# Second cross attention: score products first, three pieces, and the values of a step in one product

## The chip, the core and the metric

The kernel runs on one core of a Trainium2 chip. The metric is the time of one execution on the device, in microseconds; lower is better. The core has a matrix engine (TensorE, PE in the profile; its weight loads are listed apart as PEld), VectorE (DVE), ScalarE (ACT), GpSimd (POOL) and SyncE (SP, which issues transfers). Each runs its own instructions in order and waits for the others through semaphores. TensorE writes its results into PSUM, eight banks of 512 float32 columns on 128 partitions.

## What is computed

The reference is a decoder of two layers on 2048 rows of 256 numbers, with a context of 1601 rows of 192. Each layer has self attention, cross attention to the context and a feed-forward part, each followed by a layer norm of the sum. The change concerns the cross attention of the second layer:

```python
q = x @ w_q + b_q
k = context @ w_k + b_k
v = context @ w_v + b_v
q = q.reshape(B, Lq, N_HEADS, HEAD)   # 16 heads of 16
...
scores = jnp.einsum('bqhd,bkhd->bhqk', q, k) * scale
weights = jax.nn.softmax(scores, axis=-1)
out = jnp.einsum('bhqk,bkhd->bqhd', weights, v).reshape(B, Lq, D)
return out @ w_o + b_o
```

## The kernel before

The stages run one after the other; the second cross attention is `l1_cross_heads` (line 1105). It treats the 16 heads as 8 pairs and the 2048 queries as two halves, which makes 16 "halves" `u`, each for two heads and 1024 queries. A half runs through 13 steps `kt`, one for each block of up to 128 context rows. The two heads of a pair lie in partitions 0 to 63 and 64 to 127 of the stacked queries and keys `sq` and `sk`, so products of the two heads use different halves of TensorE's rows.

A softmax needs the maximum of each row of scores first. The kernel computes the scores twice: once with queries on the partitions, in pieces of 400 or 402 columns that VectorE reduces to a negative maximum, and once transposed, with the context on the partitions and the negative maximum as one more row of the stacked queries, so that ScalarE can take the exponential directly. The pieces of a half are computed during the half before it. A step of the loop thus has this work:

- two score products (`scores`, line 1371), one for each group of 512 queries, each of two matmuls (one per head), into two buffers `pST` of two banks each;
- two exponentials by ScalarE (line 1552) from `pST` into `pr`, which has three buffers;
- the value product of the step before (`values`, line 1386): four matmuls of 32 columns of weights, which stand side by side in the array and add into one bank `pO`;
- four or five score pieces (`maximum`, line 1319), each into one of the three banks `pM`, each reduced by VectorE (line 1433). 64 pieces belong to a half; the first step of a half has four, the others five. They run ahead by 64 + 12 pieces, so the last half and the end of the one before have none left;
- now and then a full-array unit, which uses all rows and columns and also takes a bank `pM`: the projections of the second half of the queries and keys (line 1296, in halves 4 and 5; ScalarE copies them at line 1534 and VectorE subtracts at line 1424), one normalisation per half (transposes at line 1331, in the step `kt` = 3), transposes and products of the output projection (lines 1341 and 1350), and a transposition of the maxima (`shift`, line 1325), which stands among the pieces and after which SyncE moves the row into the stacked queries.

Nothing is scheduled at run time. `units_in` (line 1123) gives the units of a step and their order, and TensorE, VectorE and ScalarE all go through the same lists. Every unit has a number in this order, its bank is the number modulo 3, and TensorE waits, before it writes a bank, until the unit three numbers before has been read out:

```python
def unit(name):
    if number[name] >= 3:
        pe_.wait_ge(s_free[number[name] % 3], number[name] // 3)
```

Because engines run in order, whatever stands behind such a wait in TensorE's program waits as well. The order of a step on TensorE is written out at the end of the tensor block: the first score product, two pieces, the second score product, the first 256 columns of the values, two pieces, the other 256 columns, the full-array units, the remaining pieces.

The first cross attention (`l0_cross_heads`) has the same plan with 8 pairs of heads of 64; its value product (line 930) has 512 columns and two column tiles of 64.

Of the kernel before, what the change touches and what calls it, by code (L numbers as in the profile page):

```python
# [1104 lines left out]
def l1_cross_heads(nc, A, G, sems):  # L1105

    H, HD, W = 16, 16, 32
    KV = CTX + 1
    ROWS = 64
    STEPS = NC_  # L1110
    HALVES = H
# [10 lines left out]
    def maxima_in(u, kt):  # L1122

        before = done(u, kt - 1) if kt else done(u - 1, STEPS - 1)
        return range(before, done(u, kt))

    def units_in(u, kt):

        whole = []
        if u == 4 and kt >= 6 and kt % 2 == 0:  # L1130
            whole.append(("q", 1, kt // 2 - 3))
        if u == 5 and kt < 8 and kt % 2 == 0:
            whole.append(("k", 1, kt // 2))
        if u >= 1 and kt == 3:
            whole.append(("norm", u - 1))
        if 9 <= u < 13 and kt in (5, 7, 9):
            whole.append(("turn", 0, u - 9) if kt == 5 else ("out", 0, u - 9, (kt - 7) // 2))
        if u == HALVES - 1 and kt >= 5 and kt < 11:
            whole.append(("turn", 1, kt // 8) if kt in (5, 8) else ("out", 1, kt // 8, (kt - 6) % 3))
        parts = []  # L1140
        for i in maxima_in(u, kt):
            parts.append(("max", i))
            if i % MX == 5 and i > MX:
                parts.append(("shift", i // MX - 1))
        if u == HALVES - 2 and kt == STEPS - 1:
            parts.append(("shift", HALVES - 1))
        return parts[:2], parts[2:4], whole, parts[4:]

    def units_of(u, kt):

        return [name for names in units_in(u, kt) for name in names]
# [14 lines left out]
    with ExitStack() as ctx:  # L1166
# [6 lines left out]
        v1 = m.sb("x1v", [P, NC_, H, W])  # L1173
# [5 lines left out]
        pr = [m.sb(f"x1pr{i}", [P, 4, QG]) for i in range(3)]  # L1179
# [11 lines left out]
        pO = m.ps("x1pO", [P, QG])  # L1191
        s_in, s_wq, s_bias, s_wv, s_one, s_vset = m.sem("x1_in"), m.sem("x1_wq"), m.sem("x1_bias"), m.sem("x1_wv"), m.sem("x1_onesrow"), m.sem("x1_vset")
        s_full, s_free = [m.sem(f"x1_slotfull{i}") for i in "012"], [m.sem(f"x1_slotfree{i}") for i in "012"]
        s_st, s_ex, s_pv, s_oc = m.sem("x1_scores"), m.sem("x1_exp"), m.sem("x1_values"), m.sem("x1_outcopied")
# [20 lines left out]
        def rows(kt):  # L1215
            return min(P, CTX - kt * P)
# [7 lines left out]
        with nc.Block() as block:  # L1224
# [64 lines left out]
            def _(pe_):  # L1289
# [65 lines left out]
# [3 lines that stand above are left out]
                    {"q": project, "k": project, "v": project_v, "max": maximum, "shift": shift, "norm": norm,  # L1358
                     "turn": turn, "out": out}[name[0]](name)

                def scores(u, kt, g):
                    if kt == 0 and g == 0:
                        pe_.wait_ge(s_sh, 32 * (u + 1))
                    q, k = sq[u // 2 % 2], sk[u // 2 % 2]
                    c = (u % 2) * 1024 + g * QG
                    n = 2 * (u * STEPS + kt) + g
                    if n >= 2:
                        pe_.wait_ge(s_ex, n - 1)
                    for a in range(2):
                        part = slice(64 * a, 64 * a + ROWS)  # L1370
                        mm = nc.tensor.matmul(pST[n % 2][0:rows(kt), a, :], k[part, kt * P:kt * P + rows(kt)],  # L1371
                                              q[part, c:c + QG], start=True, stop=True)
                    mm.then_inc(s_st, 1)

                def values(n, part):
                    u, kt = n // STEPS, n % STEPS
                    c = slice(256 * part, 256 * part + 256)
                    pe_.wait_ge(s_ex, 2 * n + 2)
                    if kt == 0:
                        if u == 0:  # L1380
                            pe_.wait_ge(s_vset, 2 + NC_)
                        else:
                            pe_.wait_ge(s_oc, u)
                    r = rows(kt)
                    for q4 in range(4):
                        mm = nc.tensor.matmul(pO[W * q4:W * q4 + W, c], v1[0:r, kt, u // 2 * 2 + q4 // 2, :],  # L1386
                                              pr[n % 3][0:r, q4, c], start=(kt == 0 and part == 0),
                                              stop=(kt == STEPS - 1 and part == 1))
                    if part == 1:
                        mm.then_inc(s_pv, 1)  # L1390

                for name in first + first_maxima:
                    unit(name)
                for u in range(HALVES):
                    for kt in range(STEPS):
                        front, middle, whole, rest = units_in(u, kt)
                        scores(u, kt, 0)
                        for name in front:
                            unit(name)
                        scores(u, kt, 1)  # L1400
                        if u or kt:
                            values(u * STEPS + kt - 1, 0)
                        for name in middle:
                            unit(name)
                        if u or kt:
                            values(u * STEPS + kt - 1, 1)
                        for name in whole + rest:
                            unit(name)
                values(HALVES * STEPS - 1, 0)
                values(HALVES * STEPS - 1, 1)  # L1410
                for name in last:
                    unit(name)

# [1 line left out]
            def _(dve):  # L1415
# [61 lines left out]
                def added(name):  # L1477
                    _, half, c, b = name
                    t = 4 * c + 2 * b
                    wait_filled(dve, name)  # L1480
                    if half == 0:
                        dve.wait_ge(s_res, t + 2)
                    else:
                        wait_emptied(dve, ("out", 0, c, b))
                    both = G.xN[:, t:t + 2, :].rearrange("p t d -> p (t d)")
                    emptied(nc.vector.tensor_tensor(both, bank(name)[:, :], both, ALU.add), name)
# [38 lines left out]
            def _(act):  # L1525
# [35 lines left out]
                def turned_rows(name):  # L1561
                    _, half, c = name
                    wait_filled(act, name)
                    if half or c >= 2:
                        wait_filled(act, ("out", half, c - 2, 1) if c >= 2 else ("out", 0, c + 2, 1))
                    emptied(nc.scalar.activation(turned[c % 2][:, :], bank(name)[:, :], ACT.Copy), name)
# [1424 lines left out]
```

## Time and profile before

| | us |
|---|---|
| median of 3 runs | 3449.01 |
| lowest and highest run | 3447.76, 3451.31 |
| the profiled execution, first to last instruction | 3459.0 |
| TensorE busy (share of the span) | 3138.3 (91%) |
| VectorE busy | 2354.6 (68%) |
| ScalarE busy | 1708.5 (49%) |
| GpSimd busy | 1731.8 (50%) |

The profile is of one execution on the chip. Its page gives busy times and the costliest groups of instructions; the trace behind it can be asked for the timeline of a stretch, the waits (who waited for whom) and the busy times of each engine in a stretch. L1319 is line 1319 of the kernel. A row of the timeline merges neighbouring instructions of the same kind: "2.50 DVE ... x5" are five instructions that took 2.50 us from the start of the first to the end of the last. In brackets stands how long the engine was idle before, and what it waited for; "issue" is time in which it waited for nothing that the profile shows. A matmul in float32 is recorded as two. The ends of matmuls are modelled, so starts are the safer marks.

### The profile page before, as it was taken

Reading aid. Unit: us, or ns where it says so; the run is one execution under the profiler, and the core shown is the slowest. Engines: PE = TensorE matmul, PEld = TensorE weight load, DVE = VectorE, ACT = ScalarE, POOL = GpSimd, SP = SyncE. Lnnn points to the kernel's source line nnn. Section 1 sums busy time; section 2 is a strip of 40 time slices with the busy share of each in tenths; the row PEclk is TensorE's granted clock in tenths of the full one; section 3 lists DMA queues with packets and bytes.
Section 4 is the critical chain, followed back from the end, with each engine's and each line's share of the span. In section 5 each row is a group of like instructions: output and inputs, shape, how many; then the busy total and the mean of one; then the engine's idle time right before and its main releaser. Section 6 shows DMA issues by size and latency. Waiting matters only on the chain. (4 is left out here: it accounts for less than half of the span.)

```text
span 3459.0 us, 62575 instructions
## 1 busy us (share of the span) xinstructions
PE 3138.3 (91%) x24201; PEld 1810.0 (52%) x24201; DVE 2354.6 (68%) x4987; ACT 1708.5 (49%) x2102; POOL 1731.8 (50%) x1163
## 2 busy tenths in 40 slices
PE   7999999989999999999999953958989999999797
PEld 3666666644555555555555523846654434444346
DVE  5999999945655665566656556156429978888518
ACT  3888888823434444444444441222234656666641
POOL 5999999814777777777777831322460000000012
PEclk9999999989999999999999976988997999999898
DMA  2000000020000000000000054730021111120101
GB/s 70 6 2 2 2 2 2 26 55 1 4 1 4 1 4 4 1 4 1 4 1 1 1 160 136 239 86 1 1 43 18 18 18 18 18 26 10 33 1 37
DMA packets 65530, 91.51 MB, mean 26 GB/s; under 512 B 9586, under 2 KB 55539, under 8 KB 64371
## 3 DMA queue, kind: packets, MB, share of 16 engines
q1 hardware_dynamic: 61682, 83.17, 9.5%
q0 software_dynamic: 3072, 4.34, 0.7%
q8 instruction: 194, 3.18, 0.4%
q14 instruction: 70, 0.57, 0.1%
q10 hardware_dynamic: 512, 0.26, 0.0%
HBM read 62.34 MB, written 10.65 MB: 21 GB/s over the span
## 5 line engine op out<-in xcount | busy, mean ns | idle before, releaser
L969 DVE TENSOR_REDUCE x0hm<-x0pM 128x1 f32<-128x400 f32 (+1 forms) x1024 | 520.8, 563 | 378.3 <-PE x0pM L871 378.2
L434 POOL TENSOR_SCALAR rows<-rows,mb 128x1024 bf16<-128x1024 bf16 x512 | 567.5, 1119 | 98.1 <-DVE mb L382 98.1
L376 DVE TENSOR_SCALAR_CACHE_REDUCE rows<-pS 128x1024 bf16<-128x1024 f32 x512 | 605.8, 1209 | 2.0 <-PE pS L312 1.5
L445 ACT ACTIVATE prT<-pP 128x1024 bf16<-128x1024 bf16 x512 | 521.9, 1024 | 110.1 <-PE pP L323 92.6
L1433 DVE TENSOR_REDUCE x1hm<-x1pM 128x1 f32<-128x400 f32 (+1 forms) x1024 | 519.1, 567 | 67.4 <-PE x1pM L1319 64.2
L1552 ACT ACTIVATE x1pr<-x1pST 128x1024 f32<-128x1024 f32 (+1 forms) x416 | 403.8, 1022 | 216.1 <-PE x1pST L1371 216.0
L831 POOL TENSOR_TENSOR x0acc<-x0acc,x0pr 128x1024 f32<-128x1024 f32 (+1 forms) x176 | 422.1, 2398 | 110.2 <-ACT x0pr L1080 95.0
L831 POOL TENSOR_TENSOR x0acc<-x0acc,o_nat 128x1024 f32<-128x1024 f32 (+1 forms) x176 | 419.1, 2381 | 72.3 <-ACT o_nat L1080 53.5
L1080 ACT ACTIVATE x0pr<-x0pST 128x1024 f32<-128x1024 f32 (+1 forms) x208 | 212.9, 1024 | 279.6 <-PE x0pST L915 279.6
L1080 ACT ACTIVATE o_nat<-x0pST 128x1024 f32<-128x1024 f32 (+1 forms) x208 | 213.0, 1024 | 278.4 <-PE x0pST L915 278.0
L2666 POOL MEMSET f_tri<- 128x128 f32 x1 | 0.2, 209 | 675.7 <-POOLq L1224 675.7
L1319 PE MATMUL x1pM<-x1sk,x1sq 64*128 64x400 f32 (+1 forms) x1024 | 322.1, 443 | 15.0 <-DVE x1ql L1424 4.1
L323 PE MATMUL pP<-ident_b,rows 128*128 128x128 bf16 x4096 | 318.8, 221 | 0.9 <-ACT prT L445 0.5
L323 PEld LDWEIGHTS pP<-ident_b,rows 128*128 128x128 bf16 x4096 | 231.1, 98 | 116.5 <-POOL rows L434 86.0
L871 PE MATMUL x0pM<-x0kh,x0qh 64*128 64x400 f32 (+1 forms) x1024 | 279.7, 368 | 11.5 <-ACT x0v L1090 4.0
L1319 PEld LDWEIGHTS x1pM<-x1sk,x1sq 64*128 64x128 f32 x1024 | 153.6, 191 | 228.1 <-issue 143.7
L1386 PE MATMUL x1pO<-x1pr,x1v 128*32 128x256 f32 (+1 forms) x3328 | 264.2, 393 | 0.4 <-ACT x1pr L1552 0.4
L1371 PE MATMUL x1pST<-x1sq,x1sk 64*128 64x512 f32 (+1 forms) x832 | 258.2, 447 | 3.1 <-ACT x1pr L1552 1.6
L312 PE MATMUL pS<-kT,qT 64*128 64x512 bf16 x1024 | 200.5, 389 | 45.2 <-DVE rows L376 30.0
L915 PE MATMUL x0pST<-x0qh,x0kh 64*128 64x512 f32 (+1 forms) x832 | 222.6, 448 | 0.0
L930 PE MATMUL x0pO<-x0pr,x0v 128*64 128x512 f32 (+1 forms) x832 | 210.8, 604 | 0.1
L930 PE MATMUL x0pO<-o_nat,x0v 128*64 128x512 f32 (+1 forms) x832 | 210.6, 604 | 0.0
(367 smaller groups left out, 5125.2 us busy)
## 6 DMA issues: line engine op xcount, KB each, us to landing
m_w<-in_moe_w1T SPq DMA_DIRECT2D x16, 1024.0 KB
m_w<-in_moe_w2T SPq DMA_DIRECT2D x16, 1024.0 KB, 9.1
acc_d<-m_zero SPq DMA_DIRECT2D x8, 514.0 KB, 9.5
m_acc<-acc_d SPq DMA_DIRECT2D x8, 514.0 KB, 5.6
x1sq<-x1qh SPq DMA_DIRECT2D x32, 128.0 KB, 4.0
x1sk<-x1kh SPq DMA_DIRECT2D x32, 100.1 KB, 3.6
rows_d<-m_xr SPq DMA_DIRECT2D x1, 2176.0 KB, 9.0
g_xN<-in_x SPq DMA_DIRECT2D x1, 2048.0 KB
```

Source lines behind the costliest of these rows:

```text
L323: mm = nc.tensor.transpose(pP[half][:, k, :], rows[u][:, kt * P:(kt + 1) * P], G.ident_b[:, :])
L376: nc.vector.tensor_scalar(rows[u][:, half * 1024:(half + 1) * 1024], pS[half][:, :], 1.0, None, ALU.mult, ALU.max, accum_out=mx[u][:, half ...
L434: nc.gpsimd.tensor_scalar(r, r, -1.0, mb[u][:, 0:1], ALU.mult, ALU.add).then_inc(s_df, 1)
L445: nc.scalar.activation(prT[u][:, half * 8:(half + 1) * 8, :], pP[half][:, :, :], ACT.Exp, scale=-1.0 / HD ** 0.5).then_inc(s_ex, 1)
L831: nc.gpsimd.tensor_tensor(total[0:r, :, :], total[0:r, :, :], pr[n % NP][0:r, :, :], ALU.add)\
L871: filled(nc.tensor.matmul(bank(name)[:, 0:w], qh[g % 3][half, t * P:(t + 1) * P], kh[g // 4 % 2][half, c0:c0 + w], start=True, stop=True), ...
L930: mm = nc.tensor.matmul(pO[64 * a:64 * a + 64, :], v_all[0:r, kt, c:c + HD], pr[n % NP][0:r, a, :], start=(kt == 0), stop=(kt == NK - 1))
L969: emptied(nc.vector.tensor_reduce(hm[g % 2][:, a, t, i % 8 // 2:i % 8 // 2 + 1], bank(name)[:, 0:w], AX.X, ALU.max, negate=True), name)
L1080: nc.scalar.activation(pr[n % NP][0:r, :, :], pST[n % 2][0:r, :, :], ACT.Exp, scale=HD ** -0.5)\
L1319: filled(nc.tensor.matmul(bank(name)[:, 0:w], q[part, c:c + P], k[part, c0:c0 + w], start=True, stop=True), name)
L1433: emptied(nc.vector.tensor_reduce(hm[u % 2][:, a, t, i % 8 // 2:i % 8 // 2 + 1], bank(name)[:, 0:w], AX.X, ALU.max, negate=True), name)
L1552: nc.scalar.activation(pr[step % 3][0:r, g::2, :], pST[n % 2][0:r, :, :], ACT.Exp, scale=HD ** -0.5).then_inc(s_ex, 1)
```

## The change

On TensorE a step becomes: both score products, three pieces, the full-array units, the values of the step before in one product of 512 columns, the remaining pieces. The order of the units in a step, and with it the banks and the order on VectorE and ScalarE, changes accordingly: a full-array unit now comes after the third piece of its step and not after the fourth.

```diff
@@ units_in
-        return parts[:2], parts[2:4], whole, parts[4:]
+        return parts[:3], whole, parts[3:]
@@ tensor block
-                def values(n, part):
+                def values(n):
                     u, kt = n // STEPS, n % STEPS
-                    c = slice(256 * part, 256 * part + 256)
                     pe_.wait_ge(s_ex, 2 * n + 2)
...
                     for q4 in range(4):
-                        mm = nc.tensor.matmul(pO[W * q4:W * q4 + W, c], v1[0:r, kt, u // 2 * 2 + q4 // 2, :],
-                                              pr[n % 3][0:r, q4, c], start=(kt == 0 and part == 0),
-                                              stop=(kt == STEPS - 1 and part == 1))
-                    if part == 1:
-                        mm.then_inc(s_pv, 1)
+                        mm = nc.tensor.matmul(pO[W * q4:W * q4 + W, :], v1[0:r, kt, u // 2 * 2 + q4 // 2, :],
+                                              pr[n % 3][0:r, q4, :], start=(kt == 0), stop=(kt == STEPS - 1))
+                    mm.then_inc(s_pv, 1)
...
-                        front, middle, whole, rest = units_in(u, kt)
+                        front, whole, back = units_in(u, kt)
                         scores(u, kt, 0)
-                        for name in front:
-                            unit(name)
                         scores(u, kt, 1)
-                        if u or kt:
-                            values(u * STEPS + kt - 1, 0)
-                        for name in middle:
+                        for name in front + whole:
                             unit(name)
                         if u or kt:
-                            values(u * STEPS + kt - 1, 1)
-                        for name in whole + rest:
+                            values(u * STEPS + kt - 1)
+                        for name in back:
                             unit(name)
-                values(HALVES * STEPS - 1, 0)
-                values(HALVES * STEPS - 1, 1)
+                values(HALVES * STEPS - 1)
```

## Rows read from the trace of the kernel before

**Rows 1.** The page, its first line.
```profile
span 3459.0 us, 62575 instructions
```

**Rows 2.** Busy times of a quiet stretch: us, busy us (x instructions), PEclk, DMA, GB/s.
```profile
2880.00:2930.00 50.00, 49.27 (x445) 20.73 (x444) 45.17 (x96) 34.28 (x36) 0.00 (x0) 1.00 0.14 19
```

**Rows 3.** The page's groups: line engine op, out<-in, count | busy us, mean ns | idle.
```profile
L1433 DVE TENSOR_REDUCE x1hm<-x1pM 128x1 f32<-128x400 f32 (+1 forms) x1024 | 519.1, 567 | 67.4 <-PE x1pM L1319 64.2
L1552 ACT ACTIVATE x1pr<-x1pST 128x1024 f32<-128x1024 f32 (+1 forms) x416 | 403.8, 1022 | 216.1 <-PE x1pST L1371 216.0
...
L1386 PE MATMUL x1pO<-x1pr,x1v 128*32 128x256 f32 (+1 forms) x3328 | 264.2, 393 | 0.4 <-ACT x1pr L1552 0.4
...
L930 PE MATMUL x0pO<-x0pr,x0v 128*64 128x512 f32 (+1 forms) x832 | 210.8, 604 | 0.1
```

**Rows 4.** Timeline of an ordinary step: start us, us, what [idle before <-releaser].
```profile
2901.65 0.19 PEld L1319 LDWEIGHTS x1pM<-x1sk,x1sq 64*128 64x128 f32 x2 [0.41 <-issue]
...
2902.02 0.16 PEld L1386 LDWEIGHTS x1pO<-x1pr,x1v 128*32 128x32 f32 x8 [0.19 <-issue]
...
2902.13 2.50 DVE L1433 TENSOR_REDUCE x1hm<-x1pM 128x1 f32<-128x400 f32 x5 [0.27 <-PE x1pM L1319]
2902.59 0.18 PEld L1319 LDWEIGHTS x1pM<-x1sk,x1sq 64*128 64x128 f32 x1 [0.41 <-issue]
...
2903.24 0.18 PEld L1319 LDWEIGHTS x1pM<-x1sk,x1sq 64*128 64x128 f32 x1 [0.30 <-DVE x1hm L1433]
...
2903.32 1.94 ACT L1552 ACTIVATE x1pr<-x1pST 128x1024 f32<-128x1024 f32 x2 [0.84 <-PE x1pST L1371]
2903.85 0.16 PEld L1386 LDWEIGHTS x1pO<-x1pr,x1v 128*32 128x32 f32 x8 [0.32 <-issue]
...
2904.41 0.19 PEld L1319 LDWEIGHTS x1pM<-x1sk,x1sq 64*128 64x128 f32 x2 [0.41 <-issue]
```

**Rows 5.** Waits in the loop: engine line <- releaser, us in total, times, longest.
```profile
PEld x1pM L1319 <- issue: 143.4, 353, 0.8
...
DVE x1hm L1433 <- PE x1pM L1319: 53.3, 191, 1.4
PEld x1pM L1319 <- DVE x1hm L1433: 41.4, 132, 0.6
...
PEld x1pST L1371 <- DMA x1sq<-x1nt: 4.3, 11, 1.6
```

**Rows 6.** Timeline of a value product of the first cross attention.
```profile
1502.61 0.20 PEld L930 LDWEIGHTS x0pO<-x0pr,x0v 128*64 128x64 f32 x4 [0.76 <-issue]
...
1503.62 0.19 PEld L915 LDWEIGHTS x0pST<-x0qh,x0kh 64*128 64x128 f32 x2 [0.81 <-issue]
```

**Rows 7.** Timeline around a projection of queries (line 1296).
```profile
2795.93 0.19 PEld L1319 LDWEIGHTS x1pM<-x1sk,x1sq 64*128 64x128 f32 x2 [0.41 <-issue]
...
2796.88 0.30 PEld L1296 LDWEIGHTS x1pM<-g_xT,x1wq 128*128 128x128 f32 x2 [0.41 <-issue]
...
2798.79 0.18 PEld L1319 LDWEIGHTS x1pM<-x1sk,x1sq 64*128 64x128 f32 x1 [0.76 <-issue]
...
2800.49 0.18 PEld L1319 LDWEIGHTS x1pM<-x1sk,x1sq 64*128 64x128 f32 x1 [1.41 <-DVE x1ql L1424]
...
2801.68 0.19 PEld L1319 LDWEIGHTS x1pM<-x1sk,x1sq 64*128 64x128 f32 x2 [0.41 <-issue]
```

**Rows 8.** Timeline around a normalisation unit (line 1331).
```profile
2709.99 0.18 PEld L1319 LDWEIGHTS x1pM<-x1sk,x1sq 64*128 64x128 f32 x2 [0.41 <-issue]
...
2712.76 0.19 PEld L1319 LDWEIGHTS x1pM<-x1sk,x1sq 64*128 64x128 f32 x2 [0.41 <-issue]
...
2713.71 0.42 PEld L1331 LDWEIGHTS x1pM<-ident,x1oc 128*128 128x128 f32 x4 [0.41 <-issue]
...
2714.29 0.18 PEld L1319 LDWEIGHTS x1pM<-x1sk,x1sq 64*128 64x128 f32 x1 [0.17 <-issue]
...
2716.41 0.19 PEld L1319 LDWEIGHTS x1pM<-x1sk,x1sq 64*128 64x128 f32 x2 [0.41 <-issue]
```

## The prediction

> **What bounds the kernel now.** I read the page first: one core, 3459.0 us from first to last instruction [rows 1]. The change touches only the loop of the second cross attention, 16 halves of 13 steps, 208 steps, so everything below is about those. Second came the busy times of a quiet stretch of it: TensorE 49.3 of 50 us, VectorE 45.2, ScalarE 34.3, granted clock 1.00 [rows 2]. TensorE looks like the bound, but the reader should not stop there. Third, the page's groups give the durations of single instructions [rows 3], and fourth, the timeline of one ordinary step shows the order in which things wait [rows 4].
>
> I call the five score pieces of a step, each reduced to a maximum by VectorE, M1 to M5; S0 and S1 are the two score products, V the value product. The old order is S0 M1 M2 S1 V M3 M4 V M5, where V stands twice, with 256 columns each. The pieces go through three PSUM banks in turn, so each piece waits until the piece three before it has been reduced: M2 waits for the previous step's M4. One loop can be followed through rows 4, a link at a time:
> - M3 and M4 are issued at 2901.65, and the first reduction starts at 2902.13: 0.48 us.
> - Five reductions in a row last 2.50 us and one lasts 0.567 [rows 3, 4], so they start (2.50 - 0.567) / 4 = 0.483 apart; M4 is reduced 0.483 after M3 and takes 0.567.
> - M4's reduction therefore ends at 2902.13 + 0.48 + 0.57 = 2903.18, and the weight load of M2, which had idled 0.30 us for VectorE, goes at 2903.24: 0.06.
> - M2 and S1 run, and the first V is issued at 2903.85: 0.61.
> - The first V takes until 2904.41, when the next step's M3 goes: 0.56.
>
> The sum is 0.48 + 0.48 + 0.57 + 0.06 + 0.61 + 0.56 = 2.76, which is 2904.41 - 2901.65: the loop closes with nothing left over. So the step is set neither by TensorE's work nor by VectorE's (5 x 0.483 = 2.42) but by a round trip through both, with three banks. Waits of both kinds confirm it [rows 5]: VectorE waits 53.3 us for pieces, TensorE's weight loads 41.4 us for emptied banks, and 143.4 us go to turning from values to pieces.
>
> **The change, part by part.**
>
> *Values in one piece.* Sixteen weight loads and matmul records per step become eight, each with 512 columns. This operation is not in the trace for four column tiles. The nearest row is the first cross attention's value product, 512 columns on two column tiles: loaded at 1502.61, next product at 1503.62, so 1.01 us [rows 6]. Above, it costs no more than the two old pieces, 2 x 0.56 = 1.12. Below, one old piece and what the longer records add: 604 ns against 393 [rows 3], two behind each other in a column tile, so 0.56 + 2 x 0.21 = 0.98. I take 1.01, since that row has the same columns, the same rows and the same two records per tile. Per step 0.11 us of TensorE is saved.
>
> *Both score products first, three pieces, then values, then two pieces.* The new order is S0 S1 M1 M2 M3 V M4 M5. M3 takes the bank of the previous step's M5, and V stands right behind M3 in TensorE's queue. The new loop, from the same links:
> - M4 issued until its reduction starts: 0.48.
> - M5's reduction starts 0.483 later, lasts 0.567, and 0.06 on M3 may go. That is M4 to M3: 0.48 + 0.48 + 0.57 + 0.06 = 1.59. In that time TensorE does M5, S0, S1, M1 and M2. In the old step M5, S0 and M1 took 0.65 (2902.59 to 2903.24, with the wait in it) and M2 with S1 0.61, so 1.26 at most: they fit, and M3 still waits some 0.3.
> - M3 to V: as M3 and M4 to V before, 2901.65 to 2902.02, 0.37.
> - V in one piece until M4 goes: 1.01.
>
> Sum 1.59 + 0.37 + 1.01 = 2.97. The round trip now contains two reductions as before, but the whole of V instead of half of it. Another quiet step lasts 2712.76 - 2709.99 = 2.77 [rows 8]; against that the loss is 0.20 a step. VectorE idles while V runs: from the end of M5's reduction to the start of the next M4's pass 0.06 + 0.37 + 1.01 + 0.48 = 1.92 us, in which it has only M1 to M3 to reduce, 3 x 0.483 = 1.45, so some 0.5 us go idle.
>
> *How many steps.* Half 15 and the last three steps of half 14 have no pieces left (16 steps, unchanged). In the other 15 halves the first step has four pieces instead of five, so one link of 0.48 is missing, and it starts behind the wait for the shift row, with empty banks; I take its first two steps as unchanged. 208 - 16 - 30 = 162 steps x 0.20 = +32 us.
>
> *Full-array units ahead of the values.* The eight projections of queries and keys now have V behind them, so ScalarE's copy and VectorE's subtraction run beside V. Before, M3 to M3 across a projection is 2801.68 - 2795.93 = 5.75 us, 2.98 more than a plain step; TensorE's own part is 2798.79 - 2796.88 = 1.91 [rows 7]. The rest, 1.07, comes from ScalarE's copy and VectorE's subtraction, for which a piece's load idles 1.41 until 2800.49; from the projection's end that is 1.7, of which V's 1.01 and M4's 0.48 now cover nearly all: 0.9 saved, in 7 of 8 (the last key projection has 66 columns), -6 us. The 15 normalisations: M3 to M3 is 2716.41 - 2712.76 = 3.65, 0.88 over a plain step, of which TensorE's is 2714.29 - 2713.71 = 0.58 [rows 8]; VectorE's part goes beside V, and I take 0.2 of the 0.30 as saved, -3 us. The 18 units of the output projection I count at nothing, since VectorE's additions run beside values in either order; without that cover I allow what a normalisation shows, 0.30 each, 5 us, and as much the other way.
>
> *What costs nothing.* S1 stands earlier; ScalarE needs 1.94 for both exponentials of a step [rows 4] against 2.97, and the second is done before the next S1 needs its bank. The exponentials wait for values three steps back, which keep their place one step behind. SyncE's queue keeps its order: the shift unit stands behind V in its step as it did, and the row's transfer now has a step of 2.97 instead of 2.77 to hide in. It shows 4.3 us of waits today [rows 5], which may grow or vanish.
>
> *Sum.* +32 - 6 - 3 = +23 us. On the profiled execution 3459.0 + 23 = 3482; that execution lies 10 us above the median of the runs, so the median goes from 3449.0 to 3472.
>
> **The rivals.**
>
> *TensorE's work decides, and it is faster.* If M3's wait were covered, the step would be 2.76 less the 0.30 that M2's load idles and the 0.11 of V: 2.35, under VectorE's 2.42, which would then set it. 162 x 0.34 = 55 us less, and the projections' 9: 3449 - 64 = 3385. For it: rows 4 show 0.19 to 0.41 us of "issue" ahead of each change between pieces and values, four in a step, of which two go. Against it: M3 waits for M5 through a bank, and no step of the sum removes that; it decides only if M5's reduction ended more than 0.3 earlier. The Trainium skill, TensorEngine Tiling, "Key Properties", says that a change of tiling mode drains the engine; by that alone fewer changes would make the kernel faster, and the trace agrees that each change idles the loads. The trace also shows that the drained time is not what M2 waits for. Chance 0.10.
>
> *The new loop needs several steps to settle.* Each half starts with empty banks. If half of the 162 steps run ahead of the loop, the loss is 16 - 9 = 7 us, 3456, at the edge of no change. Against it: in the old order the step from the third to the fourth of a half, the one with the normalisation, is already 2.77 long [rows 8]. Chance 0.08 for this and all else within 0.2%, which is 7 us and about what a measurement of this kernel can tell.
>
> *The wait is longer still.* With V at its upper end of 1.12 the loop is 3.08, 162 x 0.31 = 50, less 9: 3490. Chance 0.05 for anything over 3488.
>
> **How the numbers follow.** The forecast has 0.77. With V at 1.01 and the units saving between nothing and 13 us (8 x 1.07 and 15 x 0.30) it gives 3468 to 3481; with V at 0.98 the step is 2.94, 162 x 0.17 = 28, less 13 and less 5 for the output projection: 3459. The range starts at the second rival's 3456 and ends at 3488, short of the third's 3490. Slower 0.77 + 0.05 = 0.82, same 0.08, faster 0.10.
>
> **What would show it.** Right: in quiet steps the pieces' reductions come in runs of five, 2.97 us apart, with a gap of 0.5 us instead of 0.27; VectorE's wait for pieces grows by about 162 x 0.20 = 32 us, while TensorE's loads wait for VectorE about as long as now, at M3 instead of M2; one value product takes 1.0 us; the stage is 20 to 25 us longer and all others keep their length. Projections are shorter by almost 1 us each. Wrong: a step below 2.77, or reductions without a gap; then M3's wait is not in the loop. A step of 2.97 with an unchanged total would mean that the units gave more than I allowed.

## The result, and the profile after

| | before | after |
|---|---|---|
| median, us | 3450.16 | 3476.86 |
| lowest and highest run | 3447.76, 3455.74 | 3474.97, 3478.85 |
| runs | 4 | 4 |
| the profiled execution: span | 3459.0 | 3474.1 |

The ratio of after to before is 1.0068, 95% interval 1.0051 to 1.0085: the change makes the kernel slower, by 18 to 29 us by this interval and by 27 us on the medians. 3472 was forecast, with a range of 3456 to 3488.

The page after, its first line and two of its groups [rows 1, 3]:

```profile
span 3474.1 us, 59231 instructions
...
L1425 DVE TENSOR_REDUCE x1hm<-x1pM 128x1 f32<-128x400 f32 (+1 forms) x1024 | 513.7, 565 | 99.0 <-PE x1pM L1319 98.2
...
L1385 PE MATMUL x1pO<-x1pr,x1v 128*32 128x512 f32 (+1 forms) x1664 | 223.4, 609 | 0.4 <-ACT x1pr L1544 0.4
```

The value product has half as many records, of 609 ns each instead of 393, as the first cross attention's 512 columns had 604. VectorE's reductions are as long as before, but the idle time in front of them has grown from 67.4 to 99.0 us. The quiet stretch [rows 2]:

```profile
2880.00:2930.00 50.00, 48.90 (x290) 20.25 (x290) 42.77 (x91) 32.97 (x35) 0.00 (x0) 1.00 0.12 17
```

TensorE is busy for 48.9 of 50 us as it was (49.3), while VectorE fell from 45.2 to 42.8. Nothing in this view tells that TensorE now waits more; that takes the timeline of an ordinary step [rows 4], with the start, the length and what the idle time before was for:

```profile
2716.14 0.16 PEld L1385 LDWEIGHTS x1pO<-x1pr,x1v 128*32 128x32 f32 x8 [0.19 <-ACT x1pr L1544]
...
2717.13 0.19 PEld L1319 LDWEIGHTS x1pM<-x1sk,x1sq 64*128 64x128 f32 x2 [0.84 <-issue]
...
2717.61 2.50 DVE L1425 TENSOR_REDUCE x1hm<-x1pM 128x1 f32<-128x400 f32 x5 [0.46 <-PE x1pM L1319]
...
2718.24 0.18 PEld L1319 LDWEIGHTS x1pM<-x1sk,x1sq 64*128 64x128 f32 x1 [0.41 <-DVE x1hm L1425]
2718.72 0.18 PEld L1319 LDWEIGHTS x1pM<-x1sk,x1sq 64*128 64x128 f32 x1 [0.30 <-DVE x1hm L1425]
2719.09 0.16 PEld L1385 LDWEIGHTS x1pO<-x1pr,x1v 128*32 128x32 f32 x8 [0.19 <-ACT x1pr L1544]
...
2720.09 0.18 PEld L1319 LDWEIGHTS x1pM<-x1sk,x1sq 64*128 64x128 f32 x2 [0.84 <-issue]
```

The new loop can be followed link by link. M4 goes at 2717.13, and the first of five reductions starts at 2717.61: 0.48. M5's reduction starts 0.483 later, takes 0.567, and M3's weight load, which idled 0.30 for VectorE, goes at 2718.72: 1.11. V goes at 2719.09: 0.37. The next M4 goes at 2720.09: 1.00. The sum is 2.96, with 2720.09 - 2717.13 = 2.96. VectorE idles 0.46 us before each five reductions, where it idled 0.27.

The waits of the loop [rows 5] (engine line <- releaser: us in total, times, longest):

```profile
PEld x1pM L1319 <- issue: 150.0, 178, 1.7
PEld x1pM L1319 <- DVE x1hm L1425: 129.6, 355, 0.8
DVE x1hm L1425 <- PE x1pM L1319: 86.2, 185, 1.2
...
PEld x1pST L1371 <- DMA x1sq<-x1nt: 8.6, 14, 2.7
```

VectorE waits for pieces 86.2 us instead of 53.3, and TensorE's weight loads wait for VectorE 129.6 instead of 41.4. The idle time for nothing ("issue") in front of pieces is 150.0 as it was 143.4, but in 178 places instead of 353: half as many value products, each with 0.84 us of it behind its loads where it was 0.41. The wait for the shift row's transfer grew from 4.3 to 8.6. The loop as a whole, from the line of the score products (count, shortest/median/longest, first to last start), before and then after:

```profile
L1371 PE MATMUL x1pST<-x1sq,x1sk x832: 383/439/793, 2627.9 to 3248.5; 64*128 64x512 f32 x154, 64*65 64x512 f32 x13
```

```profile
L1371 PE MATMUL x1pST<-x1sq,x1sk x832: 383/393/793, 2624.2 to 3266.1; 64*128 64x512 f32 x154, 64*65 64x512 f32 x13
```

It was 3248.5 - 2627.9 = 620.6 us and is 641.9, 21.3 longer. The spans of the two profiled executions differ by 15.1 only, because the other stages happen to be 6 us shorter in this one: the loop starts at 2624.2 instead of 2627.9, without any change ahead of it. The 5 us by which the medians differ beyond the loop's 21.3 are no more than the spread of the runs.

### The profile page after: what moved, and what is told of

It is laid out like the page before. It is cut to its first block and busy times, and to the rows that moved or that the text cites. A ratio compares the mean times of both kernels' runs of the same rounds, so it can differ in the third digit from the quotient of the medians.

```text
span 3474.1 us, 59231 instructions
## 1 busy us (share of the span) xinstructions
PE 3159.7 (91%) x22537; PEld 1815.2 (52%) x22537; DVE 2350.6 (68%) x4987; ACT 1709.1 (49%) x2102; POOL 1731.6 (50%) x1163
## 3 DMA queue, kind: packets, MB, share of 16 engines
q8 instruction: 181, 2.97, 0.3%
## 5 line engine op out<-in xcount | busy, mean ns | idle before, releaser
L1319 PE MATMUL x1pM<-x1sk,x1sq 64*128 64x400 f32 (+1 forms) x1024 | 355.4, 444 | 10.4 <-DVE x1hm L1425 0.3
L1319 PEld LDWEIGHTS x1pM<-x1sk,x1sq 64*128 64x128 f32 x1024 | 164.7, 191 | 308.1 <-issue 150.4
L312 PE MATMUL pS<-kT,qT 64*128 64x512 bf16 x1024 | 200.6, 389 | 45.2 <-DVE rows L376 27.7
L1385 PE MATMUL x1pO<-x1pr,x1v 128*32 128x512 f32 (+1 forms) x1664 | 223.4, 609 | 0.4 <-ACT x1pr L1544 0.4
L915 PEld LDWEIGHTS x0pST<-x0qh,x0kh 64*128 64x128 f32 (+1 forms) x832 | 107.3, 181 | 183.9 <-issue 176.0
```

The costliest lines, as they stand in the source:

```text
L915: mm = nc.tensor.matmul(pST[n % 2][0:r, a, :], k[half, :], q[half, :], start=(i == 0), stop=(i == 3))
L1319: filled(nc.tensor.matmul(bank(name)[:, 0:w], q[part, c:c + P], k[part, c0:c0 + w], start=True, stop=True), name)
```

## The experiments

The experiments test the round trip of the prediction. The rivals were that the long value product, the early score products or the place of the full-array units cost the time, or that TensorE's own work sets the step. Eight kernels ran, on two chips; ratios are to runs of the kernel before on the same chip, where its median was 3457.7 both times.

**Shorter reductions, the same TensorE work** (`e1_half_reductions`, from the changed kernel):

```diff
-                                                    bank(name)[:, 0:w], AX.X, ALU.max, negate=True), name)
+                                                    bank(name)[:, 0:200], AX.X, ALU.max, negate=True), name)
```

> The changed kernel, but each reduction reads 200 of the 400 columns of its piece; the other half of every piece is left out of the maxima. TensorE's work is untouched. Round trip through the banks: a reduction of 400 columns lasts 0.567 us and one of 64 lasts 0.22, so 200 columns last about 0.36 and start 0.28 apart; the loop becomes 0.48 + 0.28 + 0.36 + 0.06 + 0.37 + 1.01 = 2.56 us a step instead of 2.97, 162 x 0.41 = 66 us less, 3411; if TensorE's own work stops it first, at some 2.64, 53 less, 3424. Rival, the long value product and the order of the products cost TensorE time by themselves: the step stays at 2.97 and the time at 3477.

Measured: 3395.1 us, ratio 0.9821 (0.9804 to 0.9837). The timeline of an ordinary step:

```profile
2890.41 0.19 PEld L1319 LDWEIGHTS x1pM<-x1sk,x1sq 64*128 64x128 f32 x2 [0.84 <-issue]
...
2890.90 1.56 DVE L1425 TENSOR_REDUCE x1hm<-x1pM 128x1 f32<-128x200 f32 x5 [0.99 <-PE x1pM L1319]
...
2891.32 0.46 PEld L1319 LDWEIGHTS x1pM<-x1sk,x1sq 64*128 64x128 f32 x2 [0.20 <-DVE x1hm L1425]
2891.97 0.16 PEld L1385 LDWEIGHTS x1pO<-x1pr,x1v 128*32 128x32 f32 x8 [0.19 <-issue]
...
2892.96 0.18 PEld L1319 LDWEIGHTS x1pM<-x1sk,x1sq 64*128 64x128 f32 x2 [0.84 <-issue]
```

The step is 2892.96 - 2890.41 = 2.55 us, against 2.56 expected: TensorE's instructions are the same, and it became faster by 0.42 because VectorE's got shorter. V is still 0.99 and M3 to V now at most 0.65 with M2 in it. The rival, which had 3477, is out. The total fell further than expected, by 83 us and not by 66, against the 3477.7 that the kernel with a loop at 2.97 takes on the same chip in the next experiment. The score products of the loop start from 2618.7 to 3186.9 here and from 2626.6 to 3270.2 there, 568.2 and 643.6 us, so 75.4 lie in the loop: the steps that the prediction left out of its 162 gain too. The rest lies ahead of it: from the first reduction to the loop's start, the 76 pieces that run ahead take 28.3 us instead of 36.8.

**The values as two products behind each other** (`e2_two_together`, from the changed kernel, with the old function of two pieces):

```diff
-                            values(u * STEPS + kt - 1)
+                            values(u * STEPS + kt - 1, 0)
+                            values(u * STEPS + kt - 1, 1)
```

> The changed kernel, but the values go as two products of 256 columns directly behind each other. Round trip: the whole of the values is in the loop all the same, 2.97 to 3.03 us a step (the second product needs its weights again), 3477 to 3487. Rival, 512 columns on four column tiles are slow in themselves: the step comes back towards 2.77 and the time towards 3450.

Measured: 3477.7 us, ratio 1.0057 (1.0040 to 1.0074), an interval that holds the changed kernel's 1.0068. An ordinary step:

```profile
2906.08 0.19 PEld L1319 LDWEIGHTS x1pM<-x1sk,x1sq 64*128 64x128 f32 x2 [0.41 <-issue]
...
2907.67 0.18 PEld L1319 LDWEIGHTS x1pM<-x1sk,x1sq 64*128 64x128 f32 x1 [0.30 <-DVE x1hm L1430]
2908.05 0.59 PEld L1386 LDWEIGHTS x1pO<-x1pr,x1v 128*32 128x32 f32 x16 [0.19 <-ACT x1pr L1549]
...
2909.05 0.19 PEld L1319 LDWEIGHTS x1pM<-x1sk,x1sq 64*128 64x128 f32 x2 [0.41 <-issue]
```

The step is 2909.05 - 2906.08 = 2.97, and the two products together take 2909.05 - 2908.05 = 1.00 us, exactly what the one takes. So 512 columns on four column tiles are not slow, and joining the two halves gains nothing either; what counts is that the whole of the values stands in one place.

**One part of the change alone: both score products first** (`e3_scores_first`, from the kernel before):

```diff
                         scores(u, kt, 0)
-                        for name in front:
-                            unit(name)
                         scores(u, kt, 1)
+                        for name in front:
+                            unit(name)
```

> The kernel before with one part of the change alone: both score products first, then two pieces, half of the values, two pieces, the other half, as before. Round trip: the second score product no longer stands between M2 and the values, so the link of 0.61 becomes 0.37 and the loop 0.48 + 0.48 + 0.57 + 0.06 + 0.37 + 0.56 = 2.52 us; TensorE's own work may stop it at up to 2.66. 162 x 0.11 to 0.25 = 18 to 40 us less than before, 3410 to 3432. Rival, the early score products are what costs in the change, since every piece comes later: slower than before, by up to the change's 0.20 a step, up to 3482.

Measured: 3429.8 us, ratio 0.9923 (0.9906 to 0.9940). Its reductions and value products:

```profile
2904.67 6.65 DVE L1433 TENSOR_REDUCE x1hm<-x1pM 128x1 f32<-128x400 f32 x13
...
2905.18 0.16 PEld L1386 LDWEIGHTS x1pO<-x1pr,x1v 128*32 128x32 f32 x8 [0.19 <-issue]
...
2905.75 0.20 PEld L1319 LDWEIGHTS x1pM<-x1sk,x1sq 64*128 64x128 f32 x2 [0.41 <-issue]
...
2907.72 0.16 PEld L1386 LDWEIGHTS x1pO<-x1pr,x1v 128*32 128x32 f32 x8 [0.19 <-issue]
...
2908.29 0.21 PEld L1319 LDWEIGHTS x1pM<-x1sk,x1sq 64*128 64x128 f32 x2 [0.41 <-issue]
```

From one first half of the values to the next is 2907.72 - 2905.18 = 2.54, from one M3 to the next 2908.29 - 2905.75, the same. VectorE does 13 reductions in 6.65 us without a gap. This part of the change alone is a gain of 0.8%, 28 us on the medians, within the 18 to 40 expected: it takes the second score product out of the loop.

**A new order that shortens the loop** (`e4_piece_between_scores`, from the kernel before):

```diff
-        return parts[:2], parts[2:4], whole, parts[4:]
+        return parts[:1], parts[1:2], parts[2:3] + whole, parts[3:]
...
+                        one, two, three, rest = units_in(u, kt)
+                        for name in one:
+                            unit(name)
                         scores(u, kt, 0)
+                        for name in two:
+                            unit(name)
                         scores(u, kt, 1)
+                        for name in three:
+                            unit(name)
                         if u or kt:
                             values(u * STEPS + kt - 1, 0)
+                        for name in rest:
+                            unit(name)
                         if u or kt:
                             values(u * STEPS + kt - 1, 1)
```

> A new order: M1 S0 M2 S1 M3, full-array units, first half of the values, M4 M5, second half. Round trip: M3 waits for M5, and only half of the values and none of the score products stand between M3 and the next M4: 0.48 + 0.48 + 0.57 + 0.06 + 0.37 + 0.56 = 2.52 us a step, up to 2.66 if TensorE's own work stops it; with the 9 us for the full-array units ahead of values that is 27 to 50 us less than before, 3400 to 3423. Rival, TensorE's work sets the step: the products and the changes between kinds are those of the kernel before, so 3450.

Measured: 3413.1 us, ratio 0.9876 (0.9858 to 0.9894). This is the version that beats both kernels, with the same products in the same sizes as before.

```profile
2904.90 6.65 DVE L1435 TENSOR_REDUCE x1hm<-x1pM 128x1 f32<-128x400 f32 x13
...
2906.97 0.19 PEld L1319 LDWEIGHTS x1pM<-x1sk,x1sq 64*128 64x128 f32 x2 [0.41 <-issue]
...
2909.52 0.19 PEld L1319 LDWEIGHTS x1pM<-x1sk,x1sq 64*128 64x128 f32 x2 [0.41 <-issue]
```

The step is 2909.52 - 2906.97 = 2.55. VectorE again runs without a gap that the view shows, one reduction per (6.65 - 0.567) / 12 = 0.507 us, but that is more than the 0.483 of [rows 4], so it is not what sets the step. TensorE's loads hardly wait for it any more, 1.2 us in the 50 from 2880 to 2930:

```profile
PEld x1pM L1319 <- DVE x1hm L1435: 1.2, 4, 0.4
```

The last experiment measures 2.54 for TensorE's own time with the products and turns of the kernel before. That this is what sets the 2.55 here is argued from the two numbers; a shorter round trip would then gain little more.

**The full-array units behind the values again** (`e5_units_behind`, from the changed kernel):

```diff
-        return parts[:3], whole, parts[3:]
+        return parts[:3], parts[3:3], whole + parts[3:]
...
-                        front, whole, back = units_in(u, kt)
+                        front, none, back = units_in(u, kt)
...
-                        for name in front + whole:
+                        for name in front:
```

> The changed kernel with the full-array units behind the values, ahead of the remaining pieces, as they were before the change. If the units gave what the prediction says (0.9 us for seven projections, 0.2 for fifteen normalisations, their copies and subtractions running beside the values), this kernel is about 9 us slower than the changed one, ratio to the kernel before about 1.0095 instead of 1.0068, with plain steps at 2.97. Rival, the place of the units is worth nothing: ratio 1.0068 again and the projection's steps as in the changed kernel.

Measured: 3493.2 us, ratio 1.0097 (1.0074 to 1.0120), as expected: 0.0029 above the changed kernel's is 10 us. M3 to M3 across a projection of queries, here and then in the changed kernel:

```profile
2802.08 0.18 PEld L1319 LDWEIGHTS x1pM<-x1sk,x1sq 64*128 64x128 f32 x1 [0.30 <-DVE x1hm L1425]
...
2803.45 0.30 PEld L1296 LDWEIGHTS x1pM<-g_xT,x1wq 128*128 128x128 f32 x2 [0.84 <-issue]
...
2808.03 0.18 PEld L1319 LDWEIGHTS x1pM<-x1sk,x1sq 64*128 64x128 f32 x1 [0.30 <-DVE x1hm L1425]
```

```profile
2799.65 0.18 PEld L1319 LDWEIGHTS x1pM<-x1sk,x1sq 64*128 64x128 f32 x1 [0.30 <-DVE x1hm L1425]
2800.13 0.30 PEld L1296 LDWEIGHTS x1pM<-g_xT,x1wq 128*128 128x128 f32 x2 [0.30 <-DVE x1hm L1425]
...
2804.71 0.18 PEld L1319 LDWEIGHTS x1pM<-x1sk,x1sq 64*128 64x128 f32 x1 [0.30 <-DVE x1hm L1425]
```

Behind the values it takes 2808.03 - 2802.08 = 5.95 us, 2.98 more than a plain step, exactly the extra of the kernel before [rows 7]; ahead of them 2804.71 - 2799.65 = 5.06, 2.09 more. So 0.89 a projection comes from their place. The loop as a whole is 656.5 us against 641.9:

```profile
L1371 PE MATMUL x1pST<-x1sq,x1sk x832: 383/393/792, 2626.1 to 3282.6; 64*128 64x512 f32 x154, 64*65 64x512 f32 x13
```

That is 14.6 where 9 were expected. The other 5 lie in the 26 steps with the projections, which take 2891.64 - 2786.73 = 104.91 us from V to V, against 2877.78 - 2784.48 = 93.30 in the changed kernel: 11.6 more, where seven projections and two normalisations make 6.6. TensorE's granted clock shows a cause. It was 1.00 in all of these steps in the changed kernel; here it fell to 0.50, the lower of its two levels (1.2 GHz), from 2854 to 2860 and, as in this line, behind the third projection:

```profile
2827.00:2833.00 6.00, 6.00 (x27) 2.01 (x19) 3.12 (x7) 1.93 (x2) 0.00 (x0) 0.50 0.02 4
```

In that stretch a value product takes 2832.90 - 2831.04 = 1.86 us instead of 1.00. So I put the 5 us down to the clock in this one execution and not to the place of the units; the ratio, which rests on four runs, shows the 10 us.

**The second score product back among the pieces** (`e6_scores_apart`, from the changed kernel):

```diff
                         scores(u, kt, 0)
+                        for name in front[:2]:
+                            unit(name)
                         scores(u, kt, 1)
-                        for name in front + whole:
+                        for name in front[2:] + whole:
                             unit(name)
```

> The changed kernel with the second score product back between the second and the third piece; the values stay in one product behind the third. Round trip: M4 to M3 stays 1.59 us, since all that TensorE does in it fits, so 2.97 a step and the changed kernel's ratio to the kernel before, 1.0068 within 0.002. Rival, the place of the score products matters in this order too, as it did with the values in two halves: 0.1 to 0.2 a step either way, 16 to 32 us.

Measured: 3474.0 us, ratio 1.0047 (1.0031 to 1.0063).

```profile
2896.47 0.16 PEld L1385 LDWEIGHTS x1pO<-x1pr,x1v 128*32 128x32 f32 x8 [0.20 <-ACT x1pr L1546]
...
2898.59 0.18 PEld L1319 LDWEIGHTS x1pM<-x1sk,x1sq 64*128 64x128 f32 x1 [0.64 <-DVE x1hm L1427]
...
2899.07 0.18 PEld L1319 LDWEIGHTS x1pM<-x1sk,x1sq 64*128 64x128 f32 x1 [0.18 <-DVE x1hm L1427]
...
2899.45 0.16 PEld L1385 LDWEIGHTS x1pO<-x1pr,x1v 128*32 128x32 f32 x8 [0.20 <-ACT x1pr L1546]
```

From one V to the next is 2899.45 - 2896.47 = 2.98, as in the changed kernel, and M3, with M2 and the score product 0.48 ahead of it, still goes 0.38 before V. The ratio is 0.0021 below the changed kernel's 1.0068, just beyond the 0.002 I allowed, and 1.0068 lies outside this interval, though the two intervals overlap. The profiles show no gain in the steps: from the second V of the loop up to the one at 3230.75, near the end of half 14, every distance from V to V is the changed kernel's within 0.02 us. Only from there to the last V it is shorter, 3266.14 - 3230.75 = 35.39 against 3267.94 - 3230.70 = 37.24; there the granted clock of the changed kernel's profile fell to 0.50 (3238 to 3241) and here it stayed at 1.00. So the place of the second score product, worth 0.8% with the values in two halves, leaves the step as it is here: between M4 and M3 the score product has room, and between M2 and the values it had none.

**TensorE's own time for both orders** (`e7_few_columns_after` and `e8_few_columns_before`): the reductions read 64 columns.

```diff
-                                                    bank(name)[:, 0:w], AX.X, ALU.max, negate=True), name)
+                                                    bank(name)[:, 0:64], AX.X, ALU.max, negate=True), name)
```

> The changed kernel with reductions of 64 columns only; the other columns are left out of the maxima. A reduction of 64 columns lasts 0.22 us and the next starts 0.14 later, so the round trip would be 0.48 + 0.14 + 0.22 + 0.06 + 0.37 + 1.01 = 2.28 us. What the plain step then lasts is that or TensorE's own time for this order. If the change saves TensorE the 0.11 us of the prediction, it lies at least 0.11 under that of the next kernel; rival, the new order saves TensorE nothing: the two are equal.

> The kernel before with reductions of 64 columns only; the other columns are left out of the maxima. The round trip would be 0.48 + 0.14 + 0.22 + 0.06 + 0.61 + 0.56 = 2.07 us a step, so the plain step shows TensorE's own time for the old order, between 2.35 and 2.66. Rival, TensorE's own time was the bound all along: 2.77 as before.

Measured, in one execution each: 3351.2 us for the new order, 3408.2 for the old one. The loads of pieces and values of a step, first the new order, then the old:

```profile
2900.13 0.19 PEld L1319 LDWEIGHTS x1pM<-x1sk,x1sq 64*128 64x128 f32 x2 [0.84 <-DVE x1hm L1425]
...
2901.40 0.16 PEld L1385 LDWEIGHTS x1pO<-x1pr,x1v 128*32 128x32 f32 x8 [0.19 <-issue]
...
2902.40 0.19 PEld L1319 LDWEIGHTS x1pM<-x1sk,x1sq 64*128 64x128 f32 x2 [0.84 <-DVE x1hm L1425]
```

```profile
2900.32 0.16 PEld L1386 LDWEIGHTS x1pO<-x1pr,x1v 128*32 128x32 f32 x8 [0.31 <-issue]
...
2900.89 0.19 PEld L1319 LDWEIGHTS x1pM<-x1sk,x1sq 64*128 64x128 f32 x2 [0.41 <-issue]
...
2902.86 0.16 PEld L1386 LDWEIGHTS x1pO<-x1pr,x1v 128*32 128x32 f32 x8 [0.32 <-issue]
...
2903.43 0.19 PEld L1319 LDWEIGHTS x1pM<-x1sk,x1sq 64*128 64x128 f32 x2 [0.41 <-issue]
```

The new order takes 2902.40 - 2900.13 = 2.27 us a step, of which V, from 2901.40, is 1.00; that is the round trip as it was expected (2.28), and TensorE's own time is as long or less. The old one takes 2903.43 - 2900.89 = 2.54 (2902.86 - 2900.32 from V to V), well above its round trip of 2.07, and none of its loads shown here waits for VectorE, so there TensorE's own time sets the step. The change does save TensorE at least 0.27 us a step, and the kernel gets slower all the same.

## Why the prediction was right

- **What bounds the kernel.** The round trip set the step before. With 200 fewer columns per reduction, the changed order went where its round trip says, and with 64 the old order came down from 2.77 to 2.54 with TensorE's work untouched. One reading was wrong: the 143.4 us of "issue" ahead of pieces are not turning from values to pieces. This idle time of the weight loads is 0.41 us behind a value product of 256 columns and 0.84 behind one of 512, so most of it is the time in which that product still runs.
- **The new loop.** Forecast 0.48 + 1.11 + 0.37 + 1.01 = 2.97; measured 0.48 + 1.11 + 0.37 + 1.00 = 2.96. The value product came out as the row with two column tiles had it. That joining its halves saves 0.11 was wrong in its reason: two halves behind each other also take 1.00, so what is saved is the turn to the pieces and back.
- **How many steps.** The sum for the loop was +23, measured +21.3. Over thirteen steps with one normalisation and no other unit the loss is 1.98 us (2745.51 - 2706.55 = 38.96 from V to V, before 2743.60 - 2706.62 = 36.98); the sum had 32 - 3 = 29 over 15 halves, 1.93. That hides an error: the steps at the start of a half, which I took as unchanged, are not. The third V of half 2 comes 5.45 us after the first where it came 5.16 (starts at 2704.07 and 2709.52, before 2704.26 and 2709.42). A plain step loses 0.19, a little less than the 0.20 of the sum, which offsets a part. And the third step from the end of half 14, which the sum counts among those without pieces, still has three.
- **Projections and normalisations.** 0.9 each was forecast for a projection and 0.89 measured. The 26 steps with the projections are even 97.37 - 93.30 = 4.07 us shorter than before (2780.60 to 2877.97 before), 8.0 less than 1.98 for each thirteen of them would make, where 6 was forecast. Not all of that is the change's: in the profile of the kernel before, the granted clock fell to 0.50 behind the last projection of queries.

```profile
2828.00:2834.00 6.00, 6.00 (x19) 2.02 (x11) 1.54 (x3) 1.38 (x3) 0.00 (x0) 0.50 0.00 0
```

  Seven times 0.89 is 6.2, so by this estimate up to 1.8 us of the loop's difference are the clock's, and the 1.8 at the end of the changed kernel's loop, against `e6_scores_apart`, offset them. For a normalisation 0.2 was forecast; the timeline after shows V to V across one, and the plain step behind it:

```profile
2709.52 0.16 PEld L1385 LDWEIGHTS x1pO<-x1pr,x1v 128*32 128x32 f32 x8 [0.19 <-ACT x1pr L1544]
...
2712.59 0.42 PEld L1331 LDWEIGHTS x1pM<-ident,x1oc 128*128 128x128 f32 x4 [0.30 <-DVE x1hm L1425]
...
2713.18 0.16 PEld L1385 LDWEIGHTS x1pO<-x1pr,x1v 128*32 128x32 f32 x8 [0.17 <-ACT x1pr L1544]
...
2716.14 0.16 PEld L1385 LDWEIGHTS x1pO<-x1pr,x1v 128*32 128x32 f32 x8 [0.19 <-ACT x1pr L1544]
```

  With the unit's load at 2712.59, 0.59 ahead of V, it is 3.66 against 2.96, 0.70 more, where it was 0.88: 0.18.
- **The signs.** VectorE's wait for pieces grew by 33 us, 32 forecast; its gap is 0.46, forecast 0.5. That TensorE's loads would wait about as long as now was wrong: 129.6 us against 41.4, since M2 waits 0.41 as well as M3 0.30. I had compared M3's release with TensorE's work for the whole stretch and not looked at M2, which waits for M4 in the new order too. It costs nothing, as M3 would wait in any case.
- **The rivals.** TensorE's work is smaller by more than the 0.11 that the first rival took off for V, 0.27 at least, and still does not decide. The second, a loop that needs some steps to settle, did not show: in half 2 the V of the third step already comes 2709.52 - 2706.55 = 2.97 after that of the second. The third needed a value product of 1.12, which it is not.

The Trainium skill, TensorEngine Tiling (Array Packing), "Key Properties", says that a change of tiling mode drains TensorE. The runs fit that: an order with two changes fewer needs at least 0.27 us less of the engine's time a step, though its score products also stand side by side and the parts were not measured apart. They also show that this is time of the engine, which reaches the kernel only where the engine's time sets the step.

## What to carry to other kernels

Where an engine looks 98% busy and another 90%, look for a loop of waits through both and add its links up; if they give the step exactly, only what shortens a link helps, and a saving of the engine's own time does not. With a ring of few buffers, look at which instructions stand between the release of a buffer and the refill that releases the next: putting a long product there whole, rather than half, cost more than the turns that it saved. The order of the same products in the same sizes was worth 1.8% here, from 1.0057 (`e2_two_together`) to 0.9876 (`e4_piece_between_scores`). And a difference of a few us between two profiles may be TensorE's clock: compare the granted clock of the same steps before explaining it.

## What the runs showed of the hardware

With two turns fewer between the row-tiled pieces and the column-tiled values, and with the score products side by side, TensorE's own step fell by at least 0.27 us (2.54 against 2.27); from the value product alone I had read 0.11. How much of it is the turns was not measured apart. And a float32 value product of 512 columns takes as long as two of 256 behind each other, 1.00 us, although the two load twice as many weights: behind a product of the same tiling, the second one's loads added nothing to the time here. In some profiles the granted clock fell from 1.00 to 0.50 for a stretch of this loop, at different places in different kernels; at 0.50 a value product took 1.86 us instead of 1.00 (`e5_units_behind`). What makes it fall is not shown here.
